# A graph layer's mask stage: VectorE's one-hots ahead of its weighting of rows, and its selecting product run by column, then chunk

## The reference, cut to what matters

```python
def _denoise_gcn_layer(x, row, col, noise, nbW, nbb, selfW, selfb, attW, attb):
    f1 = x[row]
    f2 = x[col]
    h1 = jax.nn.relu(f1 @ nbW + nbb)
    h2 = jax.nn.relu(f2 @ selfW + selfb)
    log_alpha = jnp.concatenate([h1, h2], axis=1) @ attW + attb
    u = jnp.clip(noise, EPS_NOISE, 1.0 - EPS_NOISE)
    gate = jax.nn.sigmoid(jnp.log(u) - jnp.log1p(-u) + log_alpha)
    mask = jnp.clip(gate * (ZETA - GAMMA) + GAMMA, 0.0, 1.0)[:, 0]
    rowsum = jax.ops.segment_sum(mask, row, num_segments=N_NODES) + EPS_DEG
    d_inv_sqrt = jnp.clip(rowsum ** (-0.5), 0.0, 10.0)
    vals = mask * d_inv_sqrt[row] * d_inv_sqrt[col]
    msg = vals[:, None] * f2
    return jax.ops.segment_sum(msg, row, num_segments=N_NODES)

h = jnp.maximum(_layernorm(x, axis=-1), 0.0)
x1 = _denoise_gcn_layer(h, ...)
x2 = _denoise_gcn_layer(x1, ...)
out = x + h + x1 + x2
```

## Time and profile before

| | us |
|---|---|
| median of 3 runs | 6644.3 |
| fastest and slowest of the 3 | 6623.27, 6645.11 |
| the profiled execution, its own time | 6641.64 |
| its span in the trace | 6639.7 |
| DVE busy in the span | 5275.7 (79%) |
| PE busy | 4464.0 (67%) |
| ACT busy | 2499.6 (38%) |
| POOL busy | 1104.2 (17%) |

### The profile page before, as it was taken

How to read it: one execution, slowest core, us unless ns; L and a number is a source line. 1 busy time by engine, 2 the same in 40 slices (tenths; PEclk the granted TensorE clock), 3 DMA queues, 4 the chain that set the end, 5 groups by cost and what they waited for, 6 DMA issues and landing times. The chain is left out here.

```text
span 6639.7 us, 166476 instructions
## 1 busy us (share of the span) xinstructions
PE 4464.0 (67%) x58388; PEld 4020.8 (61%) x58388; DVE 5275.7 (79%) x10519; ACT 2499.6 (38%) x5126; POOL 1104.2 (17%) x1562
## 2 busy tenths in 40 slices
PE   3777777774967777355557667967777255547776
PEld 2666666663567777344456666567777244446766
DVE  8999999995378888999966665078888899976666
ACT  2665665652344444355510000344444255520000
POOL 0000000000012222000034454012222000024544
PEclk6777777775555555677778887555555677778888
DMA  2000000001366664799979997066664799989988
GB/s 65 0 0 0 0 0 0 0 1 14 36 213 205 210 207 160 256 332 332 332 237 244 242 241 197 1 216 204 210 206 160 246 332 332 333 249 254 250 247 231
DMA packets 438062, 1160.70 MB, mean 175 GB/s; under 512 B 211241, under 2 KB 216974, under 8 KB 437402
## 3 DMA queue, kind: packets, MB, share of 16 engines
q1 hardware_dynamic: 316671, 549.99, 26.8%
q0 software_dynamic: 75264, 354.33, 19.8%
q10 hardware_dynamic: 46036, 255.30, 10.1%
HBM read 936.26 MB, written 281.94 MB: 183 GB/s over the span
## 5 line engine op out<-in xcount | busy, mean ns | idle before, releaser
L1585 PE MATMUL psG<-y_window,area 128*128 128x64 bf16 x14976 | 670.8, 217 | 779.3 <-DVE area L1233 616.5
L1585 PEld LDWEIGHTS psG<-y_window,area 128*128 128x128 bf16 x14976 | 627.2, 114 | 823.1 <-issue 511.1
L1598 PE MATMUL psG<-work,edge 112*128 112x192 bf16 x7104 | 796.2, 283 | 386.6 <-DVE edge L1268 385.4
L1598 PEld LDWEIGHTS psG<-work,edge 112*128 112x128 bf16 x7104 | 751.4, 151 | 430.5 <-DVE edge L1268 352.3
L580 POOL DMA_INDIRECT work<-msg_d,widx x444 | 536.7, 1209 | 2082.4 <-issue 1632.8
L636 ACT ACTIVATE work<-iota,work 128x149 bf16<-128x149 f32 x2496 | 789.0, 406 | 0.0
L1407 PE MATMUL psG<-area,work 128*128 128x112 bf16 x2496 | 551.5, 390 | 333.8 <-DVE area L965 333.8
L1407 PEld LDWEIGHTS psG<-area,work 128*128 128x128 bf16 x2496 | 358.0, 149 | 482.2 <-issue 338.1
L1400 PE MATMUL psG<-work,merge 128*128 128x148 bf16 x4992 | 547.2, 295 | 69.0 <-ACT work L636 69.0
L1400 PEld LDWEIGHTS psG<-work,merge 128*128 128x128 bf16 x4992 | 530.7, 132 | 91.5 <-issue 65.2
L743 ACT ACTIVATE edge<-merge,npid 128x2048 bf16<-128x2048 uint16 x156 | 313.3, 2009 | 708.1 <-DMA merge<-crel_d 708.1
(11 more groups left out here) (254 smaller groups left out, 8195.8 us busy)
## 6 DMA issues: line engine op xcount, KB each, us to landing
msg_d<-work ACTq DMA_DIRECT2D x312, 784.0 KB, 4.6
area<-rlo_d SPq DMA_DIRECT2D x312, 512.0 KB, 4.3
merge<-crel_d SPq DMA_DIRECT2D x312, 512.0 KB, 5.4
area<-crelp_d SPq DMA_DIRECT2D x312, 512.0 KB, 5.8
y_window<-y_d SPq DMA_DIRECT2D x312, 48.0 KB, 3.7
work<-msg_d,widx POOLq DMA_INDIRECT x444
y_d<-cur SPq DMA_DIRECT2D x7, 1008.0 KB, 3.8
y_d<-work SPq DMA_DIRECT2D x7, 1008.0 KB, 4.8
```

The source lines that it names most:

```text
L1585: ins = pe.matmul(psG[:, 2 * h + k // CH, k % CH * D:(k % CH + 1) * D], col_one_hots[:, h, k * P:(k + 1) * P], y_window[:, h, m * D:(m + 1 ...
L1598: ins = pe.matmul(psG[:, slot_, 0:MW], q_one_hots[slot_][0:WP, g, :, s], windows[slot_][0:WP, g, s, 0:MW], start=g == 0 and s == 0, stop=g ...
```

## The change

Two things change, both in DVE's part of the mask stage. In a step, `hots` (two steps ahead) now comes before `weigh_rows` (of the step before); the operations themselves are the same. And the selecting product of `choose` walks its three operands in another order: by tile, column and then chunk, in place of by edge (tile and chunk) and then column. It reads `h_hot` then one number after the other, where before it read it in steps of 32 bytes; it reads PSUM in steps of 24 numbers, 96 bytes, where before it read it one number after the other; and it writes `chosen` in steps of one edge's row, 112 bytes, where before it wrote 24 numbers side by side.

```diff
 def choose(p_, v):
     dve.wait_ge(gathered[0], L * T + p_ * 2 + 2)
     dve.wait_ge(hi_one_hot_ready, L * TP + p_ + 1)
-    dve.tensor_tensor(chosen[:, v, :, 0:HW].rearrange("p (u j) n -> p u j n", u=2), psG[:, 2 * v:2 * v + 2, 0:CT * HW].rearrange("p u (j n) -> p u j n", n=HW),
-                      h_hot[:, v, :, :, :].rearrange("p u n j -> p u j n"), ALU.mult).then_inc(selected[0], 1)
+    dve.tensor_tensor(chosen[:, v, :, 0:HW].rearrange("p (u j) n -> p u n j", u=2), psG[:, 2 * v:2 * v + 2, 0:CT * HW].rearrange("p u (j n) -> p u n j", n=HW),
+                      h_hot[:, v, :, :, :], ALU.mult).then_inc(selected[0], 1)
...
 def local_masks(i):
     for v in range(2):
         p_ = i * 2 + v
+        if not isinstance(i, int) or p_ + 2 < TP:
+            hots(p_ + 2, v)
         if not isinstance(i, int) or p_ > 0:
             weigh_rows(p_ - 1, 1 - v)
-        if not isinstance(i, int) or p_ + 2 < TP:
-            hots(p_ + 2, v)
         choose(p_, v)
         lo_hots(p_, v)
         if not isinstance(i, int) or p_ + 1 < TP:
             h_hots(p_ + 1, 1 - v)
```

## The result

The changed kernel takes 6478.5 us (median of 4 runs, 6465.03 to 6481.81), the kernel before 6641.65 us (median of 4, the three of the table above and one more). The ratio is 0.9756, with a 95% interval of 0.9733 to 0.9779: 163 us faster, where the forecast was 60 us faster. The direction was right, the size was not.

A forecast was written before the change was run, and what follows sets the result against it. The prediction took DVE as the bound, with idle time behind POOL. A 151.5 us saving less a 92 us loss gave -59.5 us: 6641.6 to 6582 us, forecast as 6584 with the runs' median 2.7 us higher; range 6440 to 6705 us.

The forecast's parts named there:

- What bounds the kernel: Mask stage: DVE is the bound but not full, idle 1.34 us of a 10.11 us step before `weigh_rows`, behind POOL.
- Part one, the one-hots first: Mask stage: `hots` fills DVE's wait for POOL, saving 1.01 us a step, 151.5 us over 150 steps.
- a remaining wait of 0.33 us a step: Before `weigh_rows`: one POOL instruction passes behind each of `hots`, so 0.33 of the 1.34 us wait stays.
- POOL is shut out by all of `hots`: Rival: POOL runs only after all of `hots`, the reorder saves nothing, 6736 us; chance 0.10.
- ACT's idle time for `crel_bc`: Sign in the changed profile: ACT's wait for this load falls by some 0.4 us a step.
- Part two, the product's order: Selecting product in `choose`: priced by L890, it takes 2185 ns instead of 1592, 92 us lost over 156 products.
- the prediction's line: DVE instruction price without a charge for steps: about 1.04 ns a number and 0.15 us fixed.
- the cheap write: Rival: writing `chosen` in steps costs little, product 950 ns, step 8.8 us, 6447 us; chance 0.29, wholly or in part.
- ACT's circle: Limit on the step from loading and reading `crel_bc`: 8.4 to 9.5 us, not yet binding at the forecast 9.69 us.
- the case of "faster": Whole kernel: faster by over 0.5%, from the cheap write and most of the forecast's own case; chance 0.66.

The follow-up runs named there:

- e1_order_only: The changed kernel with the old product order, so only `hots` moves ahead of `weigh_rows`: 6469.4 us, ratio 0.9752 to the kernel before.
- e4_psum: The changed kernel with the products kept in PSUM, multiplied in place and summed from there: 6414.8 us, ratio 0.9670 to the kernel before.
- e6_weigh_late: The changed kernel with `weigh_rows` behind the product instead of in front of it: 6433.3 us, ratio 0.9700 to the kernel before.

## Why the prediction was wrong, point by point

**What bounds the kernel: right.** It is DVE, with a hole of 1.34 us a step behind the chain over ACT and POOL. Filling the hole alone (`e1_order_only`) gave a ratio of 0.9752.

**Part one, the one-hots first: right in mechanism and nearly in size.** Forecast a remaining wait of 0.33 us a step because POOL is let through only behind each instruction of `hots`; the timeline shows exactly this, with 0.21 and 0.34 us in two steps. By the budget of the step it is 9.06 - 8.77 - 0.06 = 0.23 us. So part one saves 1.11 us a step by its wait and not 1.01, 166 us and not 151.5; the step of `e1_order_only` itself is shorter by 1.07 us, as its product takes 1612 ns and not 1592, and `hots` waits for its loads 6.1 us in 66 steps where it was 3.5 in 74. The rival that POOL is shut out by all of `hots` was wrong. ACT's idle time for `crel_bc` was to fall by some 0.4 us a step; it fell from 330.4 / 74 = 4.5 to 229.3 / 76 = 3.0 us, by the 1.05 us that the step has lost and 0.4 us more. The load lands sooner (median 5.0 us in place of 5.4), and what ACT no longer waits there it waits for the sum of scores, in front of L757: 84.5 / 77 = 1.1 us a step in place of 45.9 / 74 = 0.6.

**Part two, the product's order: the step that failed.** The prediction said: "I take L890, the same engine, type and nearly the same step." The step was not near enough. The term was mis-sized: 156 x 0.59 = 92 us lost, where the measured rows give 156 x 0.06 = 9 us (1651 ns in place of the 2185 forecast and the 1592 of before). L890 writes 96 bytes apart and the product 112, and the single instructions take 2052 and 1539 ns with nothing else changed (L110 and L108). That one number is 83 of the 103 us by which the forecast of the change missed; 15 us are part one's, and the rest, 5 us, is less than the spread of the runs. The rest of this part was right: what the old product paid was its read of `h_hot` in steps (L104 against L100), and reading PSUM in steps is free (L106).

One row was misread beside it. The prediction took L1007 as the price of 16-bit results 6 bytes apart. But L1007 also reads its bf16 operand 6 bytes apart. The kernel before has rows with only one of the two, and they show no price: L1004 writes 147 bf16 numbers 6 bytes apart in 294 ns, L1005 reads them so in 314 ns, and the prediction's line gives 303 ns.

```profile
L1004 DVE CAST area<-area 128x147 bf16<-128x147 f32 x1 | 0.3, 294 | 0.0
```

Why the two together take 408 ns is open. Two of the three rows that spoke against the cheap write were thus of another kind or another engine, and the forecast stood on L890 alone.

**The clue that was overlooked.** The prediction had worked out that a read in steps of 32 bytes cost 0.64 us on 768 numbers, 0.83 ns a number over the free rate, and it had a write at 1.6 ns over from L890. It took the write's price from the row whose operation was nearest, and never asked whether reads and writes in steps might cost the same. Its own argument against the write, that every result now falls in another line, held as well for the read that went away: 32 bytes apart, so does every number of `h_hot`. With the read's own price for the write, the new product would have been forecast at 1592 ns, no change, and the whole at 10.11 - 1.01 = 9.10 us a step, 6644.3 - 151.5 = 6493 us.

**The rivals.** The cheap write gave 6447 us with the bound of ACT's circle at 8.8 us; the result lies between it and the forecast. It had 0.29, "wholly or in part", and that is the case that came. Its circle was real: `e4_psum`, which frees as much of DVE as that rival did, stopped at 8.70 us, and with a second buffer more than half of the wait went.

**The numbers.** The range, 6440 to 6705 us, held the time, and the case of "faster" had 0.66. The central value lay 106 us too high: the 103 us of the change, and 2.7 us by which the median of the kernel before came out lower with its fourth run.

## What to carry to other kernels

An access in steps of 16 bytes or more through SBUF cost VectorE about the same in a read as in a write here, some 0.6 to 0.9 ns a number over the side-by-side rate (more near 96 bytes, where it was 1.4), so turning a pattern round gained nothing until the steps ended up in PSUM; and a price taken from another row needs the same step, since 96 and 112 bytes are a third apart. A wait of VectorE for GpSimd can be filled with VectorE's own work, but GpSimd was then let in only between instructions, one of its own behind each (0.24 us became 0.55), so count VectorE's instructions and not only their time. After each gain, work out which circle closes next (here a load of 5 us into one buffer with 3.9 us of reading) before freeing more of the engine.

## What the runs showed of the hardware that was not expected

- Writing float32 to SBUF in steps of 96 bytes takes 2.49 ns a number, in steps of 112 and 128 bytes 1.80 and 1.68 (L108, and L118 with (1445 - 157) / 768). Two kinds of instruction agree on it (L110 and L158, 2052 ns each).
- Writing PSUM in steps of 112 bytes costs next to nothing: 966 ns for the product from PSUM into PSUM, 957 ns for one from PSUM into SBUF with everything side by side.
- A product that takes steps through SBUF takes longer in the kernel than alone: the old one 1592 against 1522 ns, the new one 1651 against 1539 (1577 in `e6_weigh_late`). Products that take none do not: 951 and 959 ns in the kernel, 957 and 966 alone. What costs the difference is not shown.
